# Five expert tiles routed from the first three batches, ahead of the last batch's routing

## The reference

```python
logits = xf @ gate_w + gate_b                      # xf: (2048, 256) layer-normalised rows
pb = softmax(logits); _, idx = top_k(pb, 1)
weights = pb * (one-hot of idx)
def expert_step(acc, params):                      # scanned over the 8 experts
    h = gelu(xf @ w1e + b1e)                       # 256 -> 1024
    y = h @ w2e + b2e                              # 1024 -> 256
    return acc + wgt[:, None] * y, None
```

## Time and profile before

| | us |
|---|---|
| median of 3 runs | 824.59 |
| lowest and highest | 821.37, 824.75 |
| profiled execution, own time | 825.65 |
| its span in the trace | 823.8 |
| PE busy | 749.4 (91%) |
| DVE busy | 457.6 (56%) |
| ACT busy | 248.1 (30%) |
| POOL busy | 184.4 (22%) |

### The profile page before, as it was taken

The page is one execution under the profiler, slowest core; times in us unless marked ns, Lnnn a source line. Parts: engine busy times, 40 slices in busy tenths (PEclk is TensorE's granted clock), DMA queues, the critical chain, the costliest instruction groups (busy, mean ns, idle before and its releaser), DMA issues.

```text
span 823.8 us, 11156 instructions
## 1 busy us (share of the span) xinstructions
PE 749.4 (91%) x4101; PEld 580.9 (71%) x4101; DVE 457.6 (56%) x876; ACT 248.1 (30%) x454; POOL 184.4 (22%) x192
## 2 busy tenths in 40 slices
PE   5999899999989999999999999988985399999996
PEld 3766576587778878887888788855554287677675
DVE  3556579888952682368335832397897612332321
ACT  1625233132211231123122322246555032222330
POOL 2012234643000020002000200157563202122121
PEclk9979999999999999999999999989999599999999
DMA  9960800005000000000000000046013498889930
GB/s 319 386 227 1 356 1 1 0 1 204 3 1 2 2 2 2 2 2 2 2 2 2 2 2 2 2 161 261 26 52 103 158 312 285 306 289 288 307 119 13
DMA packets 21725, 86.63 MB, mean 105 GB/s; under 512 B 3229, under 2 KB 12384, under 8 KB 16352
## 3 DMA queue, kind: packets, MB, share of 16 engines
q1 hardware_dynamic: 19088, 78.18, 27.0%
q0 software_dynamic: 2560, 7.34, 2.6%
HBM read 79.22 MB, written 18.35 MB: 118 GB/s over the span
## 4 chain that ended last, share of the span: by engine, by line
PE 71%; DVE 18%; issue 6%; ACT 2%; DMA 2%; POOL 0%; SPq 0%; DVEq 0%; ACTq 0%; POOLq 0%
PE ps L1163 29%; PE ps L1906 8%; PE ps L1881 5%; PE ps L581 4%; PE ps L532 4%; PE ps L1873 3%; DVE f_ha_hi L1263 2%; DVE f_raw L1257 2%; PE ps L1315 2%; PE ps L518 2%; DVE head_max L1691 1%; PE ps L610 1%; PE ps L1450 1%; PE ps L526 1%; DVE head_sum L1700 1%
## 5 line engine op out<-in xcount | busy, mean ns | idle before, releaser
L1240 ACT ACTIVATE f_raw<-ps,cols 128x512 f32<-128x512 f32 x96 | 66.2, 690 | 250.3 <-PE ps L1163 220.4
L1163 PE MATMUL ps<-f_hb_hi,fh 128*128 128x512 f32 x256 | 101.2, 395 | 2.5 <-DVE inexact L366 2.5
L1163 PE MATMUL ps<-f_ha_hi,fh 128*128 128x512 f32 x256 | 100.0, 391 | 3.2 <-ACT f_raw L1240 3.2
L1163 PE MATMUL ps<-f_hb_lo,fh 128*128 128x512 f32 x256 | 100.4, 392 | 0.0
L1163 PE MATMUL ps<-f_ha_lo,fh 128*128 128x512 f32 x256 | 99.6, 389 | 0.0
L1263 DVE CAST f_ha_hi<-f_raw 128x512 fp32r<-128x512 f32 x64 | 32.8, 512 | 89.3 <-ACT f_raw L1240 88.2
L1906 PE MATMUL ps<-ew,hT 128*128 (+1 forms) x320 | 72.8, 381 | 2.0 <-ACT hT L1962 1.6
L1906 PEld LDWEIGHTS ps<-ew,hT 128*128 128x128 f32 (+1 forms) x320 | 52.4, 169 | 16.2 <-issue 4.2
L1066 POOL TENSOR_TENSOR rstd_all<-var_eps,const 128x4 f32<-128x4 f32 x4 | 4.1, 1036 | 244.8 <-DVE var_eps L327 244.8
L1163 PEld LDWEIGHTS ps<-f_ha_hi,fh 128*128 128x128 f32 x256 | 48.0, 188 | 14.7 <-DVE f_ha_lo L1264 4.9
L1163 PEld LDWEIGHTS ps<-f_hb_hi,fh 128*128 128x128 f32 x256 | 48.6, 190 | 13.0 <-DVE f_hb_lo L1264 2.6
(11 more groups left out here) (277 smaller groups left out, 1372.4 us busy)
## 6 DMA issues: line engine op xcount, KB each, us to landing
ew<-in_ew SPq DMA_DIRECT2D x27, 1028.0 KB, 6.7
fh<-fh_copy SPq DMA_DIRECT2D x2, 4096.0 KB, 14.1
ew<-in_ew SPq DMA_DIRECT2D x1, 8192.0 KB, 22.2
b_rows<-in_eb SPq DMA_DIRECT2D x14, 256.0 KB
fw<-fw_copy SPq DMA_DIRECT2D x3, 1024.0 KB, 6.9
x_res<-in_x SPq DMA_DIRECT2D x4, 512.0 KB, 10.9
rows<-x_res SPq DMA_DIRECT2D x4, 512.0 KB, 3.9
rows<-xn_e SPq DMA_DIRECT2D x4, 512.0 KB, 3.1
```

The source lines that it names most:

```text
L1163: ins = nc.tensor.matmul(out, *((xk, wk) if swap else (wk, xk)), start=(k == 0 and part == 0), stop=(k == w.shape[1] - 1 and part == 1))
L1240: nc.scalar.activation(f_raw[:, m % 3, :], ps[:, ring_bank(n), :], ACT.Silu if m < KH else ACT.Gelu, scale=col(("w1_s", "h1_s", "h2_s")[m ...
```

## The change

`FIRST` = 12 tiles of tokens (three batches) hold 1536 tokens. Whatever the experts, at least `EARLY` = 5 tiles of 128 can be filled from them with tokens of a single expert each, since eight experts leave at most 8 x 127 over. These five tiles get their own routing out of the counts of the first three batches. The other `LATER` = 15 tiles are routed from all counts less what the early tiles took (`e_taken`, `e_mine`). The sizes stay: 20 tiles, 7 of them paired, 27 weight loads. The order of the tiles becomes six single-expert tiles, then paired and single ones in turn (paired: 6, 8, ... 18), where before it was four and then in turn (paired: 4, 6, ... 16).

What stands where afterwards:

- TensorE: all count products of the first 12 tiles (`early_ranks`) stand ahead of `heads(LAST)` and wait for the choice of batch 2. Behind the four last projections stand 24 products for the early tokens (`slot_products`, the one-hot of places in halves of 64 columns), the counts of the last batch (`last_ranks`), and tile 0. Between `up(0)` and `columns(1)` stand 24 products for the early weights, behind `down(0)` 32 for the later tokens, and behind `down(1)` 32 for the later weights.
- VectorE: `early_places` (the counts to places, the one-hots, the experts of the five tiles) stands ahead of the last batch's residuals, `early_tokens` behind them, and the last batch's logits and choice behind that. `last_counts` stands between the copies of tiles 0 and 1, `last_places` behind tile 1's, `last_experts` and `last_tokens` behind the sum of tile 0. Statistics of batches 2 and 3 are taken tile by tile in `residual`, no longer in one run of four; the logits of batch 2 move from GpSimd to VectorE.
- ScalarE: `rows_out(1)` moves ahead of the last probabilities, `rows_out(2)` ahead of the last head copies.
- GpSimd: gathers 0 and 1 stand ahead of `rows_scale(LAST)`, gathers 2 and 3 behind it.
- SyncE: the load of expert weights 0 stands ahead of the store of the last batch's `x_res`, and load 1 ahead of the store of its normalised rows.

```diff
-RANK_AT, RANK_BANK = 2 * TT * E, (3, 4, 5, 2)
+RANKS_EARLY, RANKS_LAST, RANKS_AT, POOL_LOGITS = 5, 1, 2 * P, 7
...
+        def gather(pool, t):
+            u = t % TURN
+            if t >= TURN:
+                pool.wait_ge(e_y_out, t - TURN + 1)
+            found = rows_d2[0:FIRST * P, :] if t < EARLY else rows_d2
+            pool.indirect_dma_start(xs[:, u, :], None, found,
+                                    bass.IndirectOffsetOnAxis(ap=token_in[:, t:t + 1], axis=0))\
+                .then_inc(e_gathered[u], 16)
...  (attn1_gpsimd)
+            gate_logits(slice(0, 2 * TT))
             rows_scale(2)
-            gate_logits(2)
+            pool.wait_ge(rows_stored, 16 * 2 * LAST)
+            pool.wait_ge(placed, 2)
+            gather(pool, 0)
+            gather(pool, 1)
             rows_scale(LAST)
+            gather(pool, 2)
+            gather(pool, 3)
+
+        def slot_products(bank, tiles, hot, parts, n):
+            for t in range(tiles.start, tiles.stop):
+                for h in range(2):
+                    ins = nc.tensor.matmul(bank[half_rows(h), :], g_lo_hot[:, t, :],
+                                           hot[:, t, parts, h * n:(h + 1) * n],
+                                           start=(t == tiles.start), stop=(t == tiles.stop - 1))
+            ins.then_inc(route_full, 1)
...  (attn1_tensor, the end)
             probabilities(LAST, 0, 8)
-            pe.wait_ge(consts_ready, 7)
-            ranks_inside(0)
+            pe.wait_ge(consts_ready, 8)
+            early_ranks()
             heads(LAST)
-            ranks_before(1)
-            ranks_inside(1)
-            for j in range(TT):
-                project(LAST, j)
-            ranks_before(2)
-            ranks_inside(2)
-            ranks_before(LAST)
-            ranks_inside(LAST)
+            project(LAST, 0)
+            project(LAST, 1)
+            project(LAST, 2)
+            project(LAST, 3)
+            pe.wait_ge(scalar_out, 1)
+            pe.wait_ge(tensor_in, 1)
+            slot_products(ps[:, 1, 160:160 + 2 * EARLY], slice(0, FIRST), e_hi_hot, slice(1, 3), EARLY)
+            pe.wait_ge(placed, 2)
+            last_ranks()
...  (attn1_scalar, the end)
+            rows_out(1)
             probabilities(LAST, 0, 8)
-            rows_out(1)
+            rows_out(2)
             heads(LAST)
-            rows_out(2)
+            act.wait_ge(scalar_in, 1)
+            nc.scalar.activation(e_hi_hot[:, :, 1, :], e_hi_hot[:, :, 0, :], ACT.Identity, scale=con("place", 1))\
+                .then_inc(scalar_out, 1)
             rows_out(LAST)
...  (attn1_vector and the former moe_vector, one sequence now)
+            dve.wait_ge(g_pool_own, POOL_LOGITS)
+            choose(g_order, slice(0, 2 * TT))
+            logits(2)
+            choose(g_order, slice(2 * TT, FIRST))
+            early_places()
             residual(LAST, 0)
             residual(LAST, 1)
-            choose(g_order, 2)
             residual(LAST, 2)
             residual(LAST, 3)
-            rank(1)
-            rank(2)
-            last_logits()
+            early_tokens()
+            logits(LAST)
+            choose(g_order, slice(FIRST, NT))
+            nc.vector.tensor_tensor(g_ex[:], g_e[:], spread(g_max[:], E), ALU.subtract).then_inc(scalar_in, 1)
+            columns(0)
+            weight_parts()
+            weight_rows(e_w_hot, e_hi_hot, slice(0, FIRST), EH)
+            last_counts()
+            columns(1)
+            last_places()
+            dve.wait_ge(route_full, 4)
+            weights(ps[:, 7, 0:3 * EARLY], 0, EARLY)
+            columns(2)
+            dve.wait_ge(placed, 3)
+            dve.wait_ge(rows_last, 32)
+            sums(0)
+            last_experts()
+            last_tokens()
+            weight_rows(g_w_hot, g_hi_hot, slice(0, NT), LH)
+            columns(3)
+            sums(1)
+            dve.wait_ge(route_full, 6)
+            weights(ps[:, 1, 64:64 + 3 * LATER], EARLY, LATER)
...  (moe_tensor)
             columns(0)
             up(0)
+            pe.wait_ge(c_wo_taken, NT)
+            pe.wait_ge(tensor_in, 2)
+            slot_products(ps[:, 7, 0:3 * EARLY], slice(0, FIRST), e_w_hot, slice(0, 3), EARLY)
             columns(1)
...
                 down(t)
+                if t == 0:
+                    pe.wait_ge(scalar_out, 3)
+                    pe.wait_ge(tensor_in, 3)
+                    slot_products(ps[:, 1, 0:2 * LATER], slice(0, NT), g_hi_hot, slice(1, 3), LATER)
+                if t == 1:
+                    pe.wait_ge(tensor_in, 4)
+                    slot_products(ps[:, 1, 64:64 + 3 * LATER], slice(0, NT), g_w_hot, slice(0, 3), LATER)
```

More of the change, by code:

```diff
@@ L1335, in attn1_sync, with tokens, rows @@
             rows_at = rows_d2.rearrange("(t p) d -> p t d", p=P)
-            for b in range(B):
-                tiles = slice(b * TT, (b + 1) * TT)
+            def tokens(b):
+                return slice(b * TT, (b + 1) * TT)
+            def rows(b, stored):
                 sp.wait_ge(c_wo_taken, TT * (b + 1))
-                sp.dma_start(rows_at[:, tiles, D:2 * D], x_res[:, tiles, :]).then_inc(rows_stored, 16)
+                sp.dma_start(rows_at[:, tokens(b), D:2 * D], x_res[:, tokens(b), :]).then_inc(stored, 16)
@@ new lines, in weight_rows, with weights @@
+            def weight_rows(dst, hot, tiles, n):
+                for i in range(3):
+                    ins = nc.vector.tensor_tensor(dst[:, :, i, :], hot[:, :, 0, :], spread(g_part[i][:, tiles], n),
+                                                  ALU.mult)
+                ins.then_inc(tensor_in, 1)
+            def weights(bank, first, n):
+                slots = slice(first, first + n)
+                g_order.step(nc.vector.tensor_copy(g_weights[:, :, slots], bank.rearrange("p (a m) -> p a m", a=3)))
+                g_order.step(nc.vector.tensor_tensor(weight[:, slots], g_weights[:, 2, slots], g_weights[:, 1, slots],
+                                                     ALU.add))
+                nc.vector.tensor_tensor(weight[:, slots], weight[:, slots], g_weights[:, 0, slots], ALU.add)\
+                    .then_inc(placed, 1)
@@ new lines, in attn1_vector @@
+            columns(3)
+            sums(1)
+            dve.wait_ge(route_full, 6)
+            weights(ps[:, 1, 64:64 + 3 * LATER], EARLY, LATER)
+            dve.wait_ge(placed, 7)
+            dve.wait_ge(ld_ew, 16)
+            for t in range(2, MT):
+                if t + 1 in PAIRED:
+                    add_b1(t + 1)
+                if t + 2 < MT:
+                    columns(t + 2)
+                if t + 2 in PAIRED:
+                    second_weights(PAIRED.index(t + 2))
+                sums(t)
@@ L1896, in down @@
                 n = FIRST_LOAD[t]
[L1897 removed]
+                if t == EARLY:
+                    pe.wait_ge(placed, 4)
+                e = pe.value_load(expert_of(n), min_val=0, max_val=E - 1)
                 if t >= 2:
```

594 lines of the change are left out of this document (311 added, 283 removed).

## The result

The changed kernel takes 813.36 us (median of 4 runs, 809.79 to 814.47), the kernel before 824.67 beside it (4 runs, 821.37 to 825.0): ratio 0.9864, 95% interval 0.9825 to 0.9904. The forecast was 815.0, in a range of 811.5 to 819.5. The profiled execution took 814.47 with a span of 812.6, against 825.65 and 823.8: 11.2 us less.

What follows compares the result with a forecast made beforehand. Bound: when tile 0's tokens are known (`token_in`, 648.42), then TensorE's own work. Sum: 825.65 - 11.55 (`up(1)` earlier) + 2.2 (later products) - 0.8 (gather waits) = 815.5, median 814.5; said 815.0, 8-in-10 range 811.5 to 819.5.

Steps and rivals of the forecast that it cites:

- Copies, heads, first projection: Last batch's start: ScalarE's rows of batch 2 delay the heads' copies; first projection at 628.4 against 627.20, +1.2 us.
- `early_places`: VectorE, ahead of the last residuals: 24 instructions from 625.55, 5.7 us to the experts, 6.15 to its end.
- This cover is thin: Before `up(0)`: last counts end at 643.2, 0.4 us ahead of gather 0; a quicker gather's gain would be cut off there.
- `up(0)` at 5.3 us: First expert tile: TensorE's clock drops in the idle stretch as before, so it runs 5.3 us, 644.85 to 650.15.
- rival B: More gained: clock stays up or returns sooner in `up(0)`, products hide in gaps; 813 us; chance 0.07 (811 to 812.5).
- rival A: VectorE's new queue eats half: tokens and tile 1's copy 3 to 4 us later; 819 us; chance 0.15.
- The weight-load bound: Start of `up(1)`: its weight load allows 651.57, the other bound beside the 651.9 expected from products, transposes and copy.
- Early and later products: TensorE: 24 early weight products 0.7 us before `up(1)`; two later blocks of 32 add 2.2 us with their starts.
- Rival C: Products don't overlap, each costing 0.21 us instead of 25 ns: 833.8 us; chance 0.06 for C and slower.
- 0.8 of the 1.24 gone: After `up(1)`: TensorE's two waits of 1.24 us, from one late gather (tile 4), shrink by 0.8 us.
- my signs of being wrong: Products over 0.1 us each, `up(1)` waiting for VectorE, or TensorE waiting for later tokens, experts or gathers in first seven tiles.
- GpSimd's gather: Gather 0 on GpSimd: sum keeps 1.25 us; by the port rule it might be some tenths shorter, none of it gained.

Runs made afterwards that it cites:

- a_tokens_first: Changed kernel with early place products behind the last batch's second projection and early tokens behind its first residual: 809.4 us, ratio 0.9801.
- d_first_paired: Changed kernel with early products and tokens moved forward as in a_tokens_first, and paired half-tiles ahead of full tiles; no unused products: 810.3 us, ratio 0.9837.
- a_scale_between: Changed kernel with GpSimd's 1/std of the last batch behind gather 0 instead of behind gather 1: 810.59 us, ratio 0.9809.
- a_tokens_late: Changed kernel with early tokens made behind the last batch's choice and GpSimd's 1/std ahead of any gather: 814.16 us, ratio 0.9857.
- after: The changed kernel itself, in its first measurement and profile, against the kernel before: 813.36 us, ratio 0.9864.
- d_same: The changed kernel unaltered, measured again as the measure for the last group of variants: 812.36 us, ratio 0.9848.
- a_same: The changed kernel unaltered, measured once more beside its variants: 811.57 us, ratio 0.9822.
- b_warm: Changed kernel with 90 unused products on TensorE behind the first 12 counts of the last batch: 811.06 us, ratio 0.9833.
- d_best_again: As d_first_paired, with 75 unused products behind the last batch's counts: 808.77 us, ratio 0.9806.
- b_paired_first: Changed kernel with the paired tile first in each couple of the later tiles: 813.7 us, ratio 0.9857.
- c_first_warm: As a_tokens_first, with 75 unused products on TensorE: 809.75 us, ratio 0.9812.

## Why the prediction was right, and where it was not

**The mechanism held.** The tokens of tile 0 are known from three batches, the gather and the experts move up with them, and nothing else takes the whole place of the wait. The gain is 11.3 us by the medians beside each other, 10.2 forecast by the sum (825.65 - 815.5). The sum with its shift of 1.06 gives a median of 814.4; the 815.0 that was said is half a microsecond above it.

**Copies, heads, first projection.** 626.89 against 628.4. About 1.0 us of it was there already at batch 2's projections (613.79 against 614.80) and arose in the first 15 us of the program, so it is scatter; the step itself cost 0.5 less than I had. The rest of the order of things is as written: ScalarE's rows of batch 2 (2.06 us) stand ahead of the heads' copies, and TensorE waits for these.

**`early_places`.** Forecast 5.7 us to the experts, 6.15 to its end; measured 5.3 and 5.6 (623.83 to 629.15 and 629.43). I spaced its dependent steps at up to 0.29; most stood 0.2 apart. `token_in` came 7.33 us after the first projection, against 8.15 forecast. The 0.82 for a residual isn't what its own terms give (0.41 + 1.41/4 = 0.76); they stand 0.87 to 0.89 apart.

**From the tokens to tile 0.** "This cover is thin" was the right warning with the wrong side on top. The choice came 0.6 us after where it would have been free, since the gather landed in under 5 us, not 6.1. Counted from `token_in` `up(0)` came 7.57 later instead of 8.3. a_tokens_first and d_first_paired show the price of it: of 3.3 us earlier tokens 2.1 and 2.8 arrive, as much as the choice came earlier (the 0.7 us between the two is the clock in the last projection). a_scale_between shows what stands right behind: gather, then load. a_tokens_late, 2.8 us later, lost 0.9 only: it had the 0.6 in hand, and its gather took 3.48 us where that of the changed kernel took just under 5.

**`up(0)` at 5.3 us.** This was the term with the largest error in the profiled run, +1.34. I had taken the length from the one run I saw, in which the clock came back 3.5 us into it; three runs of the same kernel gave 6.65, 5.57 and 6.62, other variants 5.25 to 6.7. The forecast named only a shorter one as possible (rival B). Both ways were open.

**`up(1)`.** 649.95 against 651.9: 23.06 us after the first projection against 23.5. It waited for VectorE's copy of tile 1's transposes, which followed the products and transposes at once, as in the sum; VectorE had stood idle for 2.96 us ahead of it, so its new queue (rival A) didn't hold this copy up. From the end of `up(0)` it took 1.51 us. The forecast's own terms for this (0.7 and 0.85 behind 650.15) give 651.7, not the 651.9 that it says. The weight-load bound was near too: where `up(0)` was short (a_scale_between), the load held `up(1)` for 0.3 us.

**Early and later products.** The early weight products took about 0.5 us (0.7 forecast). The later ones stand for 2 x 0.62 = 1.23 us in their own rows, but cost more on the path: from `up(1)` to `up(4)` it is 23.47 us (649.95 to 673.42), where the steps of the kernel before (7.32 from `up(1)` to `up(2)`, 7.25 for each further one) give 21.82. So the two blocks cost 1.65 us, about 0.1 more before and behind each; I had 2.2. Rival C (each product drains first) is refuted: 16 to 20 ns each, also when there are 192 more.

**After `up(1)`.** 154.97 against 154.1 forecast. "0.8 of the 1.24 gone" failed: after shows 1.74 us of waits at gathers and behind them (0.89, 0.43, 0.42), and the profiles of the experiments from 0.3 to 2.1. I had given the short distance to gather 6; the wait stood at tile 7. Of my signs of being wrong, a wait for a gather in the first seven tiles, this profile just doesn't show it and d_same does (0.49 at tile 6). The distance between sum and gather alone doesn't set it, since the same code gives different amounts (a_same 1.46, d_same 0.91, counted in the same way). At each wait of 1.0 us and more stood a gather of 8.9 to 9.3 us, but so did one at a wait of 0.36 (b_warm, 8.91). Why it takes so long there stays open.

**What no step had.** In the changed order the last tile but one is a paired one, whose turned copies on ScalarE TensorE waits for with 0.44 us, where the other paired tiles wait 0.2; before, the last two tiles were single-expert ones. That is 0.2 us.

**GpSimd's gather.** The first gather took 1.24 us again (635.10 to 636.34), though VectorE stood idle beside it: its last step ended at 635.15 and the next began at 638.77. The same 1.24 stands in the profiles of the variants. The Trainium skill's rule on the shared port (SBUF — State Buffer, "Who interferes with whom") would have let it be shorter; the gain that I worked out from it did not come. The gathers behind it take 0.95: it is the first one in a row that is longer.

In sum, of the profiled run's 1.0 us below the forecast (814.47 against 815.5): to the tokens 1.3 us quicker than forecast and 1.0 of scatter ahead, tokens to `up(0)` 0.7 quicker, `up(0)` 1.3 longer, to `up(1)` 0.2 quicker, products 0.6 cheaper, gather waits 1.3 more, tail 0.2. The errors have both signs and cancel to nothing but the scatter, so that the total came this near is in part luck. The result lies in the forecast's own range (812.5 to 818), which had 0.64; one result doesn't say whether the chances were fair.

## What to carry to other kernels

When a wait is moved off the path, work out which of the covers behind it is thinnest, and from both sides: here choice and gather stood 0.6 us apart and the weight load not far behind, so a choice 1.2 us earlier brought 0.6, and tokens 3.3 us earlier brought 2.8 at the most, and that only because the choice moved with them. A wait of a microsecond and a half in a stretch of dense products can cost as much again: in three of the five profiles with such a wait of over 1.0 us (1.33, 1.42, 1.63, but not 1.04 and 1.26) the work behind it ran at the lower clock. Price a late transfer with both. And compare variants from an event that all share, not from the start of the program: 5 us of T0's scatter is more than any of these edits is worth.

## What was not expected of the hardware

- The granted clock returned at different times with the same instructions before it: 6.1 us into `up(0)` in one run of the changed kernel and 3.8 in another (a_same, just after 643); 3.5 in the kernel before. TensorE had then worked at the lower level all that time.
- The clock fell while TensorE was at work (b_warm, mean 0.57 from 632 to 636 with TensorE busy throughout), after a stretch with gaps of 1.06 and 1.74 us. In d_best_again it was at full level until 640 and low from 640 to 644, behind a gap of 1.9 us.
- A wait of 1.33 us for a gather between full stretches was followed by 16 products at 5.40 us instead of 3.71 (b_paired_first; likewise c_first_warm). There it made a late gather twice as dear as its row says.
- Products of 30 and 45 columns into one half of the PSUM rows and the other in turn, with a new weight load each, follow each other every 16 to 20 ns (the block of 32 as a whole cost 0.8 us on the path).
- One indirect gather of 128 rows landed after 3.48 us with little other traffic (DMA share 0.35 from 636 to 640 in a_tokens_late), after 6.12 in the kernel before, and after 8.9 to 9.4 us at the late gathers issued between 676 and 688. It isn't the place alone: one issued at 680.22 in d_first_paired took 3.6, and all from 690 to 760 in after took 3.3 to 5.8. In after the late one stood beside two weight loads of 1 MB each. What was issued between 680 and 694 in after (form, KB each, median us to landing):

```profile
ew<-in_ew SPq DMA_DIRECT2D x2, 1028.0 KB, 9.4
```
